# A perceiver block: the first key tile of a batch turned between two groups of key products, and copied ahead of the scaled probabilities

## The chip, the cores and the metric

The kernel runs on one core of a Trainium2 chip, as one program. The metric is the device time of a run in microseconds (us); lower is better. The kernel is written in five instruction streams, one for each engine (TensorE, VectorE, ScalarE, GpSimd, SyncE), which wait for one another by counting semaphores: `then_inc(s, 1)` counts up when an instruction is done, `wait_ge(s, n)` holds a stream, with all that is behind it, until the count is n.

## The reference

Three residual blocks over x (32 sequences of 32 rows, 512 wide): cross-attention to a context of 257 rows per sequence, a second attention-like block, and a mixture of 8 experts. The change touches the cross-attention alone:

```python
x = x + xattn(layernorm(x), ctx, mask, ...)
# in xattn: 8 heads of 64
q = (x @ Wq) ...; k, v = split(context @ Wkv)
q = per_head_ln(q, qn_w); k = per_head_ln(k, kn_w)
attn = softmax(where(mask, q @ k.T * SCALE, -inf))
out = (attn @ v) @ Wo
```

The kernel does not form v: it multiplies the probabilities with the context (the "context products") and applies the value weights afterwards. Products that need full precision are made from a high and a low part of each operand, three products in place of one (`split_products`).

## The kernel before

**Batches.** A batch b is one sequence, 32 in all, four to a tile of 128 rows; r is the batch's place in its tile (0 to 3). The 257 context rows of a sequence are two key tiles of 128 and a remainder of one row, which is done for all sequences at the start. The function `batch(tile, r, ...)` exists once in each engine's stream and is called 31 times with keys to make (`main`, b = 1 to 31; batch 0 is done in the opening), and once more for the last scores. The middle six tiles are a hardware loop. An iteration b does two things at once: it makes the normalised, transposed keys kT of batch b and the second half of the work of batch b-1 (scores, softmax, context products: `prev`). It also begins the key products of batch b+1 (`nxt`). The part of an iteration on each engine is fixed by the order in which it is written; nothing is planned at run time.

**TensorE in iteration b (L1758 on)**, in order:
1. scores of batch b-1 into pS (L1774, 16 small products), after the keys kT of batch b-1 are copied (kT0_set, kT1_set, k_rem);
2. key products of batch b, tile 1, into pK1 (`k_half`, L1632; 12 products of 512 columns);
3. in r=1 only, the output products of the tile before (`out_tile`, L1730);
4. nine of the twelve key products of batch b+1, tile 0, into pK0 (L1787);
5. four transposes of the scaled probabilities of batch b-1 into pP (L1802), after ScalarE's L841 (semaphore p_n);
6. the three products left of step 4 (L1805); in r=0 two transposes of the remainder's probabilities (L1810);
7. eight transposes of the normalised keys kn of batch b, four per tile, into pT0 and pT1 (L1818), after VectorE's k_norm of tile 1 (k_n); each four count k_t up by one;
8. 24 context products of batch b-1, twelve into pP and twelve into pV1 (L1834), after the low part of the probabilities pT (p_lo, VectorE L1254).

**ScalarE in iteration b (L820 on)**: high part of the context rows (L828); two exponentials (L834); square of the key products of tile 1 (`k_square`, L730); the two scaled probabilities (L841), after VectorE's p_scale; logarithm and exponential for the key norm of tile 1 (`k_root`, L734, L736); high part of the transposed probabilities pP into pT (L849); in r=0 a copy for the remainder (L852); `keys_copy` (L724 to L726), the copy of pT0 into the first half of kT, after the first count of k_t; high part of the context of b+2 (`ctx_high`, L722); square for b+1, tile 0; a copy of the first twelve context products into z (L871); `k_root` for b+1, tile 0; in r=0 four small copies (L878).

**VectorE in iteration b (L1217 on)**: mask (L1224, writes s_m) and maximum (L1227) of the scores; a transpose of blocks of context (L1106); p_den, p_inv, p_scale (L1235 to L1239), after the exponentials; p_rem (L1243); sum of squares and norm of key tile 1 (L1111, L1117); in r=1 a copy of the output products (L1214); low part of pT (L1254); the remainder's key column (L1261) and the copy of pT1 into the second half of kT (L1156), after k_t; sum and norm of tile 0 of b+1; a copy of the last twelve context products (L1270).

**GpSimd** makes low parts of context rows (L581) and of transposed context (L591), and copies queries (L587). **SyncE** issues the loads; neither has a wait on k_t in this loop (SyncE waits for its final count once, after the last batch).

Of the kernel before, what the change touches and what calls it, by code (L numbers as in the profile page):

```python
# [15 lines left out]
P = 128  # L16
# [21 lines left out]
def perceiver_block(nc, x, ctx, mask, xWq, xWkv, xWo, qn_w, kn_w, aWq, gq, bq, mq, vq, aWk, gk, bk, mk, vk,  # L38
# [6 lines left out]
    C = D // P  # L45
    BT = P // S
    MT = M // P
# [30 lines left out]
    with ExitStack() as es:  # L78
# [22 lines left out]
        ident = sb("ident", [P, P])  # L101
# [596 lines left out]
        def _(act):  # L698
# [29 lines left out]
            def k_square(b, t):  # L728
                act.wait_ge(k_mm, b * MT + t + 1)
                act.activation(sq[:, t], pKV[t][:, :], ACT.Square).then_inc(k_sq, 1)  # L730
# [89 lines left out]
            def batch(tile, r, main=True, prev=True, nxt=True, first=False, far=True):  # L820

                b = tile * BT + r
                u, pr = r % 2, (r - 1) % BT
                if main:
                    act.wait_ge(ctx_in[u], (tile * 2 + r // 2 + 1) * 16)
                    if not first:
                        act.wait_ge(pc_mm, (b - 1) * 2)
                    act.activation(ctxN[:, u, HI], ctx_raw[:, u], ACT.Copy).then_inc(cn_hi, 1)  # L828
                if prev:
                    act.wait_ge(sc_max, b)  # L830
                    if not first:
                        act.wait_ge(p_t, b - 1)
                    for g in range(G):
                        act.activation(prob[:, g, 0:M], s_m[:, g, 0:M], ACT.Exp, bias=neg_max[:, g:g + 1],  # L834
                                       accum_out=p_sum[:, g:g + 1]).then_inc(sc_exp, 1)
                if main:
                    k_square(b, 1)
                if prev:
                    act.wait_ge(sc_step, b * 3)
                    for g in range(G):  # L840
                        act.activation(prob[:, g, 0:MT * P], prob[:, g, 0:MT * P], ACT.Copy,  # L841
                                       scale=p_scale[:, g:g + 1]).then_inc(p_n, 1)
                if not main:
                    ln_root(TILES)
                if main:
                    k_root(b, 1)
                if prev:
                    act.wait_ge(p_t, b)
                    act.activation(pT[:, HI], pP[:, :, :], ACT.Copy).then_inc(p_hi, 1)  # L849
                    if r == 0:  # L850
                        act.wait_ge(p_rt, tile)
                        act.activation(pT_rem[0:3 * B, :], pV1[0:3 * B, 0:G * P], ACT.Copy).then_inc(p_rh, 1)  # L852
                if not main:
                    ln_root(TILES + 1)
                    out_high(4)
                    bn_root(0)
                if main:
                    keys_copy(b + 1)
                if far:
                    ctx_high(b + 2, u)  # L860
                if nxt:
                    k_square(b + 1, 0)
                if main and not nxt:
                    act.wait_ge(pc_mm, (b - 1) * 2 + 2)
                    out_high(2)

                if prev:
                    if r == 1 and not first:
                        act.wait_ge(o_mm, tile)
                    act.wait_ge(pc_mm, (b - 1) * 2 + 1)  # L870
                    act.activation(z[:, 2:4, :, pr, :], prob_ctx(1), ACT.Copy).then_inc(z1_set, 1)  # L871
                if nxt:
                    k_root(b + 1, 0)
                if prev:
                    if r == 0:
                        act.wait_ge(p_rh, tile)
                        for i in range(BT):
                            act.activation(rem_b[0:3 * B, :, i, :], pT_rem[0:3 * B, :].rearrange(  # L878
                                "p (h q) -> p h q", h=H), ACT.Copy, scale=sel[0:3 * B, bass.ds((tile - 1) * BT + i, 1)]).then_inc(p_rx, 1)
# [56 lines left out]
            for n in range(3 * TILES):  # L936
                w, t = divmod(n, TILES)
# [664 lines left out]
        def _(pe):  # L1602
# [140 lines left out]
            def z_product(n):  # L1743
# [11 lines left out]
                    pe.wait_ge(z_c, n - 2)  # L1755
                split_products(pe, pZ[n % 3][:, :], rows_of(xT, t), weight(w_a[:, w % 2]), C).then_inc(z_mm, 1)

            def batch(tile, r, main=True, prev=True, nxt=True, first=False):  # L1758


                b = tile * BT + r
                u, pr = r % 2, (r - 1) % BT
                if prev:
                    pe.wait_ge(kT0_set, b)
                    pe.wait_ge(kT1_set, b)
                    pe.wait_ge(k_rem, b)
                    pe.wait_ge(q_set, b)
                    if not first:
                        pe.wait_ge(sc_m, b - 1)
                    pe.nop(nofuse=True)  # L1770
                    for c in range(C):
                        for e in range(2):
                            half = slice(e * HD, (e + 1) * HD)
                            last = pe.matmul(pS[c * S:(c + 1) * S, e, 0:M], q_b[half, 1 - u, c, :],  # L1774
                                             kT[half, c, :], start=True, stop=True, tile_position=(e * HD, c * S))
                    last.then_inc(sc_mm, 1)
                if main:
                    pe.wait_ge(k_n, b * MT)
                    if first:
                        pe.wait_ge(q_n, TILES)  # L1780
                    k_half(b, 1, u)
                if r == 1 and not first:
                    out_tile(tile - 1)
                if nxt:
                    pe.wait_ge(k_n, b * MT + 1)
                    pe.wait_ge(ctx_lo, b + 2)
                    split_products(pe, pK0[:, :], ctx_rows(1 - u, 0), wk, C - 1, stop=False)  # L1787
                if main and not nxt:
                    pe.wait_ge(k_n, b * MT + 1)
                    project(0)  # L1790
                if not main:
                    project(1)
                    project(2)
                if prev:
                    pe.wait_ge(p_n, b * G)
                    if first:
                        pe.wait_ge(rem_act, 6)
                    else:
                        pe.wait_ge(z1_set, b - 1)
                    for t in range(MT):  # L1800
                        for g in range(G):
                            last = pe.transpose(pP[:, t, g * P:(g + 1) * P], prob[:, g, t * P:(t + 1) * P], ident[:, :])  # L1802
                    last.then_inc(p_t, 1)
                if nxt:
                    split_products(pe, pK0[:, :], ctx_rows(1 - u, 0), wk, C, start=False, first=C - 1).then_inc(k_mm, 1)  # L1805
                if prev and r == 0:
                    pe.wait_ge(p_rs, b)
                    pe.wait_ge(z0_set, b - 1)
                    for g in range(G):
                        last = pe.transpose(pV1[0:3 * B, g * P:(g + 1) * P], p_rem[:, g].rearrange("p k b -> p (k b)"), ident[:, :])  # L1810
                    last.then_inc(p_rt, 1)
                if not main:
                    project(3)
                if main:
                    pe.wait_ge(k_n, b * MT + 2)
                    for t in range(MT):
                        for c in range(C):
                            last = pe.transpose(pTT[t][:, c, :], kn[:, t, c * P:(c + 1) * P], ident[:, :])  # L1818
                        last.then_inc(k_t, 1)
                if prev:  # L1820
                    pe.wait_ge(cn_lo, b)
                    pe.wait_ge(p_lo, b)
                    for g in (1, 0):
                        for j in range(2):
                            c = 2 * g + j
                            o = pC[g][:, j * G * P:(j + 1) * G * P]
                            if (g, j) == (0, 0):
                                if not first:
                                    pe.wait_ge(z0_set, b - 1)
                                    if r == 0:  # L1830
                                        pe.wait_ge(p_rh, tile)
                                    if r == 1:
                                        pe.wait_ge(o_out, tile)
                            last = split_products(pe, o, lambda s, t: ctxN[:, 1 - u, s, t, c * P:(c + 1) * P],  # L1834
                                                  lambda s, t: pT[:, s, t, :], MT)
                        last.then_inc(pc_mm, 1)
# [228 lines left out]
```

## Time and profile before

| what | value |
|---|---|
| runs | 729.49 us median of 3 (724.91, 729.49, 729.84) |
| profiled execution | 726.1 us, span 724.0 us |
| TensorE products busy | 691.9 us (96%), 4651 |
| TensorE weight loads | 566.2 us (78%) |
| VectorE | 492.2 us (68%) |
| ScalarE | 443.3 us (61%) |
| GpSimd | 315.7 us (44%) |
| chain that ended last | TensorE 76%, VectorE 7%, DMA 5%, ScalarE 4% |

The span is what the trace covers; the execution's own time is 2.1 us longer. The batch loop lies between about 65 and 440 us of the span. TensorE's clock stands at nine tenths or more in 39 of the 40 slices of the span. In the trace a matmul has two records: a weight load (PEld) and the product (PE); products are pipelined, so three that follow one another take less than three times one.

### The profile page before, as it was taken

Reading aid. Unit: us, or ns where it says so; the run is one execution under the profiler, and the core shown is the slowest. Engines: PE = TensorE matmul, PEld = TensorE weight load, DVE = VectorE, ACT = ScalarE, POOL = GpSimd, SP = SyncE. Lnnn points to the kernel's source line nnn. Section 1 sums busy time; section 2 is a strip of 40 time slices with the busy share of each in tenths; the row PEclk is TensorE's granted clock in tenths of the full one; section 3 lists DMA queues with packets and bytes.
Section 4 is the critical chain, followed back from the end, with each engine's and each line's share of the span. In section 5 each row is a group of like instructions: output and inputs, shape, how many; then the busy total and the mean of one; then the engine's idle time right before and its main releaser. Section 6 shows DMA issues by size and latency. Waiting matters only on the chain.

```text
span 724.0 us, 14037 instructions
## 1 busy us (share of the span) xinstructions
PE 691.9 (96%) x4651; PEld 566.2 (78%) x4651; DVE 492.2 (68%) x869; ACT 443.3 (61%) x936; POOL 315.7 (44%) x243
## 2 busy tenths in 40 slices
PE   5888899999999999999999999999999989999996
PEld 4666778888888887888888878888788868888875
DVE  6766786766676767767667666877468766655573
ACT  4654676775776666856667655475564545565650
POOL 1473452544443434435353434744930024555534
PEclk9999999999999999999999999999999989999999
DMA  9963535352533443434524306630126367666549
GB/s 259 206 121 99 157 74 147 73 146 72 145 109 108 104 114 94 123 91 127 141 77 116 104 1 188 212 130 8 59 65 226 115 206 209 111 116 107 104 72 345
DMA packets 95063, 91.98 MB, mean 127 GB/s; under 512 B 11440, under 2 KB 68784, under 8 KB 95024
## 3 DMA queue, kind: packets, MB, share of 16 engines
q1 hardware_dynamic: 89728, 79.14, 39.6%
q0 software_dynamic: 4720, 11.27, 8.5%
q10 hardware_dynamic: 576, 1.05, 0.4%
q8 instruction: 23, 0.38, 0.2%
q14 instruction: 16, 0.13, 0.1%
HBM read 71.52 MB, written 19.92 MB: 126 GB/s over the span
## 4 chain that ended last, share of the span: by engine, by line
PE 76%; DVE 7%; DMA 5%; SPq 4%; ACT 4%; issue 2%; POOL 2%; DVEq 0%; ACTq 0%; POOLq 0%
PE pK L33 40%; PE pV L33 10%; PE pP L33 8%; PE pV L1730 5%; PE pT L1818 4%; PE pP L1802 2%; PE pS L1774 2%; DMA mask_f<-in_mask_BxSxS_bk_dram 2%; DMA fin<-total 1%; PE pT L1963 1%; SPq L409 1%; DMA big<-x_rows,idx_x 1%; SPq L421 1%; DVE ctxR L1106 1%; POOL mask_f L577 1%
## 5 line engine op out<-in xcount | busy, mean ns | idle before, releaser
L33 PE MATMUL pK<-parts 128*128 128x512 f32 x744 | 188.5, 400 | 1.9 <-DVE kn L1117 1.0
L33 PEld LDWEIGHTS pK<-parts 128*128 128x128 f32 x744 | 134.4, 188 | 41.2 <-issue 13.6
L591 POOL TENSOR_TENSOR parts<-ctxR,parts 128x1024 fp32r<-128x1024 f32 x32 | 77.0, 2407 | 186.6 <-ACT parts L722 186.6
L581 POOL TENSOR_TENSOR parts<-big,parts 128x1024 fp32r<-128x1024 f32 x32 | 77.9, 2434 | 29.0 <-ACT parts L828 28.9
L1117 DVE TENSOR_TENSOR kn<-pK,head_rs 128x512 f32<-128x512 f32 x62 | 42.9, 692 | 40.5 <-ACT head_rs L736 40.5
L33 PE MATMUL pK<-w,lhs 128*128 x276 | 69.1, 399 | 0.5 <-DVE lhs L1539 0.2
L1111 DVE TENSOR_REDUCE head_ss<-sq 128x8 f32<-128x512 f32 x62 | 42.5, 685 | 28.7 <-ACT sq L730 28.7
L33 PEld LDWEIGHTS pK<-w,lhs 128*128 128x128 f32 x276 | 50.3, 188 | 11.4 <-issue 1.8
L834 ACT ACTIVATE prob<-s_m,neg_max 128x257 f32<-128x257 f32 x64 | 32.2, 506 | 38.1 <-DVE neg_max L1227 38.1
L33 PE MATMUL pP<-pT,parts 128*128 128x256 f32 x384 | 52.7, 286 | 0.0
L1555 DVE TENSOR_TENSOR w_p<-big,w_p 128x1024 fp32r<-128x1024 f32 x22 | 27.0, 1226 | 37.8 <-ACT w_p L1031 37.8
L33 PE MATMUL pV<-pT,parts 128*128 128x256 f32 x384 | 50.1, 279 | 0.0
L677 POOL DMA_INDIRECT total<-big,idx x20 | 31.7, 1586 | 40.9 <-ACT big L1045 40.9
L33 PEld LDWEIGHTS pP<-pT,parts 128*128 128x128 f32 x384 | 47.2, 188 | 1.8 <-issue 0.2
L33 PEld LDWEIGHTS pV<-pT,parts 128*128 128x128 f32 x384 | 47.3, 188 | 0.0
L33 PE MATMUL pK<-w_p,parts 128*128 128x512 f32 x156 | 41.0, 414 | 2.1 <-DVE w_p L1126 1.9
L33 PE MATMUL pK<-w_a,xT_hi 128*128 128x512 f32 x128 | 40.2, 395 | 0.0
L841 ACT ACTIVATE prob<-prob,p_scale 128x256 f32<-128x256 f32 x64 | 29.1, 502 | 15.8 <-DVE p_scale L1239 13.1
L849 ACT ACTIVATE pT<-pP 128x512 fp32r<-128x512 f32 x32 | 19.1, 598 | 32.0 <-PE pP L1802 32.0
L671 POOL DMA_INDIRECT big<-x_rows,idx_x x23 | 26.7, 1162 | 25.0 <-DVE idx_x L1511 10.6
L33 PEld LDWEIGHTS pK<-w_p,parts 128*128 128x128 f32 x156 | 30.0, 197 | 9.5 <-DVE w_p L1126 2.3
L1254 DVE TENSOR_TENSOR pT<-pP,pT 128x512 fp32r<-128x512 f32 x32 | 22.1, 692 | 22.3 <-ACT pT L849 20.5
(331 smaller groups left out, 1521.6 us busy)
## 6 DMA issues: line engine op xcount, KB each, us to landing
big<-in_ctx_dram SPq DMA_DIRECT2D x32, 512.0 KB, 4.7
big<-in_ctx_dram SPq DMA_DIRECT2D x120, 128.0 KB, 2.7
total<-zero SPq DMA_DIRECT2D x32, 256.0 KB, 4.8
w_raw<-in_L_ffn_w_dram SPq DMA_DIRECT2D x16, 512.0 KB, 7.0
big<-in_L_ffn_w_dram SPq DMA_DIRECT2D x8, 512.0 KB, 5.7
fin<-total SPq DMA_DIRECT2D x8, 512.0 KB, 7.7
total<-big SPq DMA_DIRECT2D x8, 256.0 KB, 2.8
x_rows<-big SPq DMA_DIRECT2D x8, 256.0 KB, 2.0
```

The lines of the kernel that those rows point to most:

```text
L33: last = pe.matmul(out, lhs(a, c), rhs(b, c), start=start and c == first and n == 0, stop=stop and c == chunks - 1 and n == 2)
L581: nc.gpsimd.tensor_tensor(ctxN[:, u, LO], ctx_raw[:, u], ctxN[:, u, HI].bitcast(F32), ALU.subtract).then_inc(cn_lo, 1)
L591: nc.gpsimd.tensor_tensor(ctxT[:, u, LO], ctxR[u][:, :, :], ctxT[:, u, HI].bitcast(F32), ALU.subtract).then_inc(ctx_lo, 1)
L671: nc.gpsimd.indirect_dma_start(xg[:, j % 2, :], None, x_rows[:, :], bass.IndirectOffsetOnAxis(idx_x[:, j:j + 1], 0), bounds_check=T - 1).t ...
L677: nc.gpsimd.indirect_dma_start(total[:, :], bass.IndirectOffsetOnAxis(idx[:, j:j + 1], 0), y_sb[:, j % 2, :], None, bounds_check=5 * T - 1 ...
L834: act.activation(prob[:, g, 0:M], s_m[:, g, 0:M], ACT.Exp, bias=neg_max[:, g:g + 1], accum_out=p_sum[:, g:g + 1]).then_inc(sc_exp, 1)
L841: act.activation(prob[:, g, 0:MT * P], prob[:, g, 0:MT * P], ACT.Copy, scale=p_scale[:, g:g + 1]).then_inc(p_n, 1)
L1111: nc.vector.tensor_reduce(head_ss[:, t], heads(sq[:, t]), AX.X, ALU.add).then_inc(k_ss, 1)
L1117: tt(heads(kn[:, t]), heads(pKV[t][:, :]), per_head(head_rs[:, t]), ALU.mult).then_inc(k_n, 1)
L1555: tt(w2_buf(j)[:, LO], w2_all[:, bass.ds(e, 1)].rearrange("p e c n -> p (e c) n"), w2_buf(j)[:, HI].bitcast(F32), ALU.subtract).then_inc(w ...
L1730: last = pe.matmul(o, weights, rows[:, e * C + c].rearrange("p b q -> p (b q)"), start=k == 0, stop=k == C, tile_position=(0, e * HD))
L1818: last = pe.transpose(pTT[t][:, c, :], kn[:, t, c * P:(c + 1) * P], ident[:, :])
```

## The change

In TensorE's stream the eight transposes of step 7 are split. A new function `keys_turn(t)` makes the four of key tile t and counts k_t up. `keys_turn(0)` now stands right behind step 2, ahead of the output products and of the nine key products, with a wait for the norm of tile 0 alone; `keys_turn(1)` stays at step 7, behind the wait for tile 1. In ScalarE's stream the copy of pT0 (`keys_copy`) moves up, from behind L849 (and L852) to between the square of tile 1 and the two scaled probabilities. Nothing else moves, and the number of instructions on each engine, leaving waits aside, is the same.

```diff
--- before.py
+++ after.py
@@ -835,6 +835,8 @@
                                        accum_out=p_sum[:, g:g + 1]).then_inc(sc_exp, 1)
                 if main:
                     k_square(b, 1)
+                if main:
+                    keys_copy(b + 1)
                 if prev:
                     act.wait_ge(sc_step, b * 3)
                     for g in range(G):
@@ -854,8 +856,6 @@
                     ln_root(TILES + 1)
                     out_high(4)
                     bn_root(0)
-                if main:
-                    keys_copy(b + 1)
                 if far:
                     ctx_high(b + 2, u)
                 if nxt:
@@ -1755,6 +1755,11 @@
                     pe.wait_ge(z_c, n - 2)
                 split_products(pe, pZ[n % 3][:, :], rows_of(xT, t), weight(w_a[:, w % 2]), C).then_inc(z_mm, 1)
 
+            def keys_turn(t):
+                for c in range(C):
+                    last = pe.transpose(pTT[t][:, c, :], kn[:, t, c * P:(c + 1) * P], ident[:, :])
+                last.then_inc(k_t, 1)
+
             def batch(tile, r, main=True, prev=True, nxt=True, first=False):
 
 
@@ -1779,6 +1784,9 @@
                     if first:
                         pe.wait_ge(q_n, TILES)
                     k_half(b, 1, u)
+                if main:
+                    pe.wait_ge(k_n, b * MT + 1)
+                    keys_turn(0)
                 if r == 1 and not first:
                     out_tile(tile - 1)
                 if nxt:
@@ -1813,10 +1821,7 @@
                     project(3)
                 if main:
                     pe.wait_ge(k_n, b * MT + 2)
-                    for t in range(MT):
-                        for c in range(C):
-                            last = pe.transpose(pTT[t][:, c, :], kn[:, t, c * P:(c + 1) * P], ident[:, :])
-                        last.then_inc(k_t, 1)
+                    keys_turn(1)
                 if prev:
                     pe.wait_ge(cn_lo, b)
                     pe.wait_ge(p_lo, b)
```

## Rows read from the trace of the kernel before

**Rows 1.** Busy time by stretch, scores to scores: r=1, r=2, r=3, r=0 (us, count, clock, DMA).

```profile
303.90:319.24 15.34, 15.34 (x157) 13.10 (x157) 9.57 (x16) 9.49 (x22) 5.21 (x4) 1.00 0.33 87
319.24:329.85 10.61, 10.61 (x78) 8.68 (x77) 7.94 (x15) 7.56 (x17) 4.95 (x4) 1.00 0.47 121
329.85:340.58 10.73, 10.73 (x77) 8.66 (x77) 7.94 (x15) 7.67 (x18) 5.06 (x4) 1.00 0.42 122
340.58:351.37 10.79, 10.79 (x80) 8.92 (x79) 7.95 (x15) 8.04 (x19) 5.06 (x4) 1.00 0.45 122
```

**Rows 2.** The list of waits, TensorE: total us, times, longest.

```profile
PE pP L1802 <- ACT prob L841: 4.8, 5, 1.7
...
PEld pP L1802 <- ACT prob L841: 12.7, 23, 2.2
...
PEld pT L1818 <- DVE kn L1117: 5.9, 17, 0.6
```

**Rows 3.** Order of time, r=1: start, us, engine, line, what, idle before.

```profile
311.97 2.34 PE L33 MATMUL pK<-parts 128*128 128x512 f32 x9
...
314.14 0.60 PE L1802 MATMUL pP<-ident,prob 128*128 128x128 f32 x4
...
314.50 0.94 PE L33 MATMUL pK<-parts 128*128 128x512 f32 x3
314.78 0.60 ACT L849 ACTIVATE pT<-pP 128x512 fp32r<-128x512 f32 x1 [3.71 <-PE pP L1802]
...
315.27 1.04 PE L1818 MATMUL pT<-ident,kn 128*128 128x128 f32 x8
315.41 0.69 DVE L1254 TENSOR_TENSOR pT<-pP,pT 128x512 fp32r<-128x512 f32 x1 [2.50 <-ACT pT L849]
...
316.25 1.65 PE L33 MATMUL pP<-pT,parts 128*128 128x256 f32 x12
```

**Rows 4.** The same view, r=3.

```profile
329.44 0.30 ACT L734 ACTIVATE head_log<-head_ss,bias 128x8 f32<-128x8 f32 x1 [0.27 <-DVE head_ss L1111]
...
329.85 0.67 PE L1774 MATMUL pS<-kT,q_b 64*32 64x257 f32 x16
...
330.44 5.05 PE L33 MATMUL pK<-parts 128*128 128x512 f32 x21
...
331.15 2.42 POOL L581 TENSOR_TENSOR parts<-big,parts 128x1024 fp32r<-128x1024 f32 x1 [0.23 <-ACT parts L828]
331.31 0.68 DVE L1224 SCALAR_TENSOR_TENSOR s_m<-mask_f,pS 128x514 f32<-128x514 f32 x1
...
333.75 0.58 ACT L730 ACTIVATE sq<-pK 128x512 f32<-128x512 f32 x1
333.88 0.16 DVE L1235 SCALAR_TENSOR_TENSOR p_den<-neg_max,p_sum 128x2 f32<-128x2 f32 x1
...
334.47 0.91 ACT L841 ACTIVATE prob<-prob,p_scale 128x256 f32<-128x256 f32 x2
...
335.43 0.66 PE L1802 MATMUL pP<-ident,prob 128*128 128x128 f32 x4
...
336.12 0.60 ACT L849 ACTIVATE pT<-pP 128x512 fp32r<-128x512 f32 x1 [0.20 <-PE pP L1802]
...
336.75 0.69 DVE L1254 TENSOR_TENSOR pT<-pP,pT 128x512 fp32r<-128x512 f32 x1
...
337.40 0.60 ACT L726 ACTIVATE kT<-pT 128x512 f32<-128x512 f32 x1 [0.68 <-PE pT L1818]
...
337.59 1.65 PE L33 MATMUL pP<-pT,parts 128*128 128x256 f32 x12
```

**Rows 5.** The same view, transposes of the probabilities in r=2 and r=0.

```profile
324.73 0.62 PE L1802 MATMUL pP<-ident,prob 128*128 128x128 f32 x4
...
346.18 0.66 PE L1802 MATMUL pP<-ident,prob 128*128 128x128 f32 x4
```

**Rows 6.** The same view, p_den of the second batch.

```profile
83.04 1.54 DVE L1235 SCALAR_TENSOR_TENSOR p_den<-neg_max,p_sum 128x2 f32<-128x2 f32 x1
```

## The prediction

> **What bounds the kernel now.** I read four views in this order: the list of waits, the busy time by stretch, the order of time in one batch of each kind, and two batches near the start. I call a batch by r, its place in its tile of four, and by b from 1 to 31; S is the start of its scores, P that of the transposes of its probabilities (L1802), C that of its context products.
>
> The stretches between the scores of four neighbouring batches last 15.34, 10.61, 10.73 and 10.79 us, with TensorE busy in all of it at the full granted clock, 1.00, the 2.4 GHz level [rows 1]. The batch r=1 is the long one, since the output products stand in it. So TensorE's queue sets the pace: a step off it pays only if it takes a wait out of it, and a step put into it costs.
>
> The waits that the change could remove are small. TensorE's products stood still before L1802 for 4.8 us in only 5 batches; its weight loads 12.7 us in 23, mostly while earlier products still ran, and 5.9 us before the key transposes [rows 2]. In r=3 the products begin at 330.44 and take 5.05; a last one that began 0.39 (the length of one) before their end would let the transposes begin 0.22 later, as in r=1 (311.97 + 2.34 - 0.39 = 313.92, transposes at 314.14). That is 335.32; they began at 335.43. So 0.11 us of real wait, though the loads show 0.36 there [rows 3, 4].
>
> The second thing to see is a race at the end of each batch. After P the probabilities go through ScalarE's copy (L849) and VectorE's low part (L1254), and only then may the context products begin. Meanwhile TensorE does three key products and all eight key transposes. In r=1: P 314.14, low part ready at 316.10 (315.41 + 0.69), context products 316.25 [rows 3]. In r=3: P 335.43, ready 337.44, products 337.59 [rows 4]. The eight transposes end just when the low part is ready: they are the cover of this chain.
>
> **The change, part by part.**
>
> *Four transposes go in front, between two groups of key products.* The kernel has the same insertion already: four transposes between nine and three products. Products cost (5.05 - 2.34) / 12 = 0.226 each, so twelve in one piece take 2.34 + 3 x 0.226 = 3.02; with the four between them they last from 311.97 to 314.50 + 0.94 = 315.44, 3.47 [rows 3, 4]. Insertion: **0.45 us**. Lower bound 0.36, start to start of the four (314.50 - 314.14); upper 0.55, if the restart is counted in full (314.50 against 311.97 + 9 x 0.22). I take 0.45, it counts both ends. Their input, the normalised tile 0, is made at the end of the batch before, and the target is free once the scores have begun: no wait is expected there. Behind them are queued, in r=1, the output products, in all batches the next tile's products, then P.
>
> The trace shows four such transposes 0.36 apart in all, about 0.09 each, plus a restart. The Trainium skill (TensorE: Matmul & The Clock Gate, Back-to-back issue gap) gives about 81 ns for a 128-column product in a stream of loads and products. By that the insertion would be estimated at 0.32 instead of 0.45; it is a rival below.
>
> *The four behind the probabilities go.* The old tail from P to C is 2.11 us in r=1 (316.25 - 314.14) [rows 3]. Eight transposes there take 316.25 - 315.27 = 0.98; four less save some 0.44, so TensorE would be ready at P + 1.67. But the low part is ready at P + 1.96 (r=1) or P + 2.01 (r=3), and the products start 0.06 to 0.10 later. I take P + 2.07. From C to the next S are 340.58 - 337.59 = 2.99, so P to S becomes 5.06. Now it is 319.24 - 314.14 = 5.10 (r=1), 329.85 - 324.73 = 5.12 (r=2), 340.58 - 335.43 = 5.15 (r=3), 351.37 - 346.18 = 5.19 (r=0) [rows 1, 3, 4, 5]. The removal gives back 0.04, 0.06, 0.09 and 0.13 only: the rest turns into a wait of the context products for pT, some 0.3 to 0.4 us in every batch.
>
> *ScalarE's copy of 0.60 us goes ahead of the scaled probabilities.* It used to wait 0.68 for TensorE and then run [rows 4]. Ahead of L841 there is a gap that hides part of it: the square starts at 333.75, L841 at 334.47, 0.72 later, of which the square itself fills some 0.57. With the copy between them L841 comes about 1.17 after the square: +0.45. Queued behind it on ScalarE are L841, the root for key tile 1 and L849; TensorE waits for L841 and then L849. Against that, with the copy gone from its old place, the next square and sum come earlier. The logarithm at 329.44 no longer waits 0.27 for the sum, and VectorE, which works through the key norm and a copy before the mask step at 331.31 (scores over at 329.85 + 0.67 = 330.52), starts that up to 0.30 earlier [rows 4]. Net on ScalarE +0.15: L841 ends at S + 5.53 + 0.15 = S + 5.68 (334.47 + 0.91 - 329.85 = 5.53). TensorE gets to P at S + 0.59 + 5.05 + 0.45 - 0.17 = S + 5.92. So TensorE decides by 0.15 to 0.2, and the copy is free; without the earlier start ScalarE would give P at S + 6.03, nearly the same. No DMA and no queue of SP or POOL is moved; POOL's low part of ctx only comes about 1 us earlier.
>
> *Sum.* P moves by +0.45 (r=1), +0.43 (r=2: 319.24 + 5.92 = 325.16 against 324.73), +0.34 (r=3: 335.77 against 335.43), +0.32 (r=0: 346.50 against 346.18) [rows 3 to 5]. Less what is given back: +0.41, +0.37, +0.25, +0.19. The 23 regular batches b = 5 to 27 hold six each of the first three and five of the last: 6 x 1.03 + 5 x 0.19 = 7.1. The eight at the ends: b=28 0.2, b=29 0.4, b=31 (no wait at P) 0.45. In b=2, 3, 30 VectorE's p_scale is late anyway (b=2: L1235 lasts 1.54 [rows 6]) and both the copy and the transposes fit into the wait: -0.05 each. In b=1 and 4 TensorE waits for L841, which comes later: 0.3 each. Together 1.5. Total **+8.6 us**.
>
> The profiled execution took 726.1 (span 724.0), so it becomes 734.7. The runs shown have the median 729.49, between 724.91 and 729.84, so the execution lies 3.4 below the median; from the middle of the runs, some 728, I come to **737 us**. Bounds: insertion 0.36 gives about +6, insertion 0.55 with no earlier start on the softmax side about +13.
>
> **Rivals.**
>
> 1. *The split costs less than its row, or the tail gives back more.* If the four cost 0.32, every P that TensorE sets moves 0.13 less, 28 x 0.13 = 3.6: +5, 733. If the low part did not hold the context products, the tail would return 0.44 per batch against 0.45 spent: +0.3, 728. For it: the work is only moved. Against it: P to ready is 1.96 and 2.01 in two kinds of batch, all of it made of instructions that the change does not touch. These two together: 0.37, both inside 1%.
>
> 2. *Faster.* The place is P: if keys ready early took away the waits before L1802 and the transposes cost nothing in the shadow of weight loads. The price at most: 4.8 us of product waits and about 0.3 per regular batch of small waits at P and at the keys, 23 x 0.3 = 7: 726.1 - 12 = 714; half of it is likelier, 720. It decides where L841 ends later than S + 5.92 now; it ends at S + 5.53. Hence 0.06. The scores' side can't be advanced much either: POOL's L581 runs until 331.15 + 2.42 = 333.57, and in b=2 a tiny VectorE step stretched to 1.54 beside it [rows 4, 6]. The Trainium skill (SBUF — State Buffer, SBUF: two separate sides) says that VectorE and GpSimd lock a shared port and the loser blocks; the trace agrees with those 1.54 us.
>
> 3. *Slower still.* ScalarE's copy catches the transposes late (they end at about S + 3.44 + 0.66 = S + 4.1, the square at 333.75 + 0.58 - 0.30, S + 4.2) or p_den, now some 0.3 earlier, lands behind POOL. Each adds 0.2 to 0.3 on L841 in the 17 batches r=2, 3, 0: +4 to +5 more, 742. Chance 0.12.
>
> The forecast itself: 0.45.
>
> **How the numbers follow.** A measurement of this kernel tells about 1%, 7.3 us, from no change. The forecast of +8.6 lies just beyond; some of its own spread falls within: 0.45 gives 0.38 slower and 0.07 same. Rival 1 gives 0.32 same and 0.05 slower, rival 3 0.12 slower, rival 2 0.06, of which 0.05 faster. Slower 0.55, same 0.40, faster 0.05. The range reaches from rival 1's lower end, 728.5, to rival 3's, 742.
>
> **What the changed profile would show.** Scores to scores near 15.75, 10.98, 10.98 and 10.98 us. Four key transposes about S + 3.4, the products after them 0.45 later. L726 on ScalarE right behind the square, without idle time. L841 near S + 4.8. L849 and L1254 as far behind P as now. Context products with a new wait for pT (L1254) of 0.3 to 0.4, which is the step that makes the loss; if that wait is missing and C follows P by 1.7, I am wrong and nothing changes. If nine products follow the first twelve with less than 0.36 between, the insertion was overpriced. If P waits for L841 by more than 0.2, rival 3 holds.

## The result, and the profile after

The changed kernel is slower, by about 1%. Its runs have the median 734.31 us against 728.79 of the runs beside them, ratio 1.0087 with a 95% interval of 1.0054 to 1.012 (the ratios in this text are not quotients of medians; that of these two is 1.0076). Two later rounds of it gave 1.0109 (1.0081 to 1.0138) and 1.0105 (1.0085 to 1.0125). The forecast was 737, with 728.5 to 742. The profiled execution has a span of 732.7 us against 724.0, +8.7, where the sum said +8.6.

First the busy time by stretch of the changed kernel, from scores to scores, r=1, 2, 3, 0; the columns are those of [rows 1].

```profile
309.06:324.74 15.68, 15.32 (x157) 13.07 (x157) 9.41 (x17) 8.98 (x21) 5.68 (x5) 1.00 0.31 84
324.74:335.79 11.05, 10.68 (x77) 8.78 (x76) 7.86 (x16) 7.41 (x17) 5.08 (x3) 1.00 0.45 118
335.79:346.85 11.06, 10.69 (x78) 8.78 (x77) 7.75 (x16) 7.46 (x17) 5.09 (x3) 1.00 0.43 119
346.85:357.80 10.95, 10.80 (x79) 8.89 (x79) 7.76 (x16) 8.06 (x19) 4.46 (x2) 1.00 0.45 119
```

Each batch is longer than in [rows 1], and TensorE is no longer busy in all of it: 0.36 or 0.37 us are missing in r=1, 2 and 3, and 0.15 in r=0. The clock is the same. The list of waits of the changed kernel (total us, times, longest) names the missing piece; L1810 is now what L1802 was, L843 what L841 was.

```profile
PE pP L33 <- DVE pT L1254: 9.4, 25, 1.0
...
PE pP L1810 <- ACT prob L843: 1.9, 2, 1.5
```

The list of the kernel before has no line like the first. The wait is 0.32 to 0.37 us in 23 batches of r=1, 2 and 3. In r=0 no such wait shows but for 0.15 us in batch 4: there two transposes of the remainder's probabilities stand in the tail as well. Before the probabilities TensorE waits less, 1.9 us in place of the 4.8 of [rows 2]. Next the order of time in r=1, which answers to [rows 3].

```profile
317.57 2.34 PE L33 MATMUL pK<-parts 128*128 128x512 f32 x9
...
319.74 0.60 PE L1810 MATMUL pP<-ident,prob 128*128 128x128 f32 x4
...
320.10 0.95 PE L33 MATMUL pK<-parts 128*128 128x512 f32 x3
320.38 0.60 ACT L851 ACTIVATE pT<-pP 128x512 fp32r<-128x512 f32 x1 [4.55 <-PE pP L1810]
...
320.89 0.60 PE L1760 MATMUL pT<-ident,kn 128*128 128x128 f32 x4
321.01 0.69 DVE L1254 TENSOR_TENSOR pT<-pP,pT 128x512 fp32r<-128x512 f32 x1 [2.50 <-ACT pT L851]
...
321.85 1.60 PE L33 MATMUL pP<-pT,parts 128*128 128x256 f32 x12 [0.36 <-DVE pT L1254]
```

The chain P, L851, L1254, context products has kept its length: 321.85 - 319.74 = 2.11, as in [rows 3]. Four transposes fewer stand in it, and the products wait for the low part instead. The last view of this kernel is r=2; it answers to [rows 4] and [rows 5].

```profile
324.74 0.66 PE L1779 MATMUL pS<-kT,q_b 64*32 64x257 f32 x16
...
325.33 3.02 PE L33 MATMUL pK<-parts 128*128 128x512 f32 x12
...
325.90 0.68 DVE L1224 SCALAR_TENSOR_TENSOR s_m<-mask_f,pS 128x514 f32<-128x514 f32 x1
...
328.19 0.60 PE L1760 MATMUL pT<-ident,kn 128*128 128x128 f32 x4
...
328.39 0.60 ACT L730 ACTIVATE sq<-pK 128x512 f32<-128x512 f32 x1
...
328.54 2.31 PE L33 MATMUL pK<-parts 128*128 128x512 f32 x9
...
328.88 0.59 ACT L726 ACTIVATE kT<-pT 128x512 f32<-128x512 f32 x1
...
329.36 0.91 ACT L843 ACTIVATE prob<-prob,p_scale 128x256 f32<-128x256 f32 x2
...
330.70 0.60 PE L1810 MATMUL pP<-ident,prob 128*128 128x128 f32 x4
...
332.80 1.65 PE L33 MATMUL pP<-pT,parts 128*128 128x256 f32 x12 [0.37 <-DVE pT L1254]
```

The 21 key products with the four transposes in them last from 325.33 to 328.54 + 2.31 = 330.85, 5.52 us against 5.05: the insertion costs 0.47. P is at S + 5.96, set by TensorE (L843 ends at 330.27, with no wait shown at P). P to context products is 2.10.

To compare kernels I also use the length of the loop in their profiles, from the scores of batch 1 to those of batch 32: 371.5 us before, 379.0 after, +7.5. The other 1.2 us of the +8.7 lie outside it: the first scores come 0.9 later (66.31 against 65.38), and what follows the loop takes 0.3 more. The loop is steadier than the whole run, for a reason given at the end.

### The profile page after: what moved, and what is told of

The parts are those of the page before. It is cut to its first block, busy times and chain, and to the rows that moved or that the text cites. A ratio compares the mean times of both kernels' runs of the same rounds, so it can differ in the third digit from the quotient of the medians.

```text
span 732.7 us, 14037 instructions
## 1 busy us (share of the span) xinstructions
PE 694.1 (95%) x4651; PEld 568.7 (78%) x4651; DVE 484.7 (66%) x869; ACT 437.3 (60%) x936; POOL 315.9 (43%) x243
## 3 DMA queue, kind: packets, MB, share of 16 engines
q10 hardware_dynamic: 576, 1.05, 0.4%
## 4 chain that ended last, share of the span: by engine, by line
PE 75%; DVE 6%; ACT 4%; SPq 4%; DMA 4%; POOL 4%; issue 2%; DVEq 0%; ACTq 0%; POOLq 0%
PE pK L33 38%; PE pV L33 11%; PE pP L33 9%; PE pV L1730 4%; DVE pT L1254 3%; ACT pT L851 3%; PE pS L1779 2%; PE pP L1810 2%; PE pT L1760 2%; DMA mask_f<-in_mask_BxSxS_bk_dram 2%; PE pT L1968 1%; SPq L409 1%; DMA big<-x_rows,idx_x 1%; SPq L421 1%; POOL mask_f L577 1%
## 5 line engine op out<-in xcount | busy, mean ns | idle before, releaser
L33 PE MATMUL pK<-parts 128*128 128x512 f32 x744 | 195.0, 404 | 0.9 <-POOL parts L591 0.9
L33 PEld LDWEIGHTS pK<-parts 128*128 128x128 f32 x744 | 132.7, 188 | 38.8 <-DVE kn L1117 7.9
L581 POOL TENSOR_TENSOR parts<-big,parts 128x1024 fp32r<-128x1024 f32 x32 | 77.8, 2431 | 52.3 <-ACT parts L828 52.3
L851 ACT ACTIVATE pT<-pP 128x512 fp32r<-128x512 f32 x32 | 19.2, 599 | 47.0 <-PE pP L1810 47.0
L1254 DVE TENSOR_TENSOR pT<-pP,pT 128x512 fp32r<-128x512 f32 x32 | 22.1, 692 | 31.4 <-ACT pT L851 31.4
L1760 PE MATMUL pT<-ident,kn 128*128 128x128 f32 x248 | 37.3, 273 | 1.0 <-DVE kn L1117 1.0
L730 ACT ACTIVATE sq<-pK 128x512 f32<-128x512 f32 x62 | 36.7, 591 | 1.5 <-PE pK L33 0.2
```

The costliest lines, as they stand in the source:

```text
L33: last = pe.matmul(out, lhs(a, c), rhs(b, c), start=start and c == first and n == 0, stop=stop and c == chunks - 1 and n == 2)
L581: nc.gpsimd.tensor_tensor(ctxN[:, u, LO], ctx_raw[:, u], ctxN[:, u, HI].bitcast(F32), ALU.subtract).then_inc(cn_lo, 1)
L1254: tt(pT[:, LO], pP[:, :, :], pT[:, HI].bitcast(F32), ALU.subtract).then_inc(p_lo, 1)
```

## Experiments

| kernel | ratio to before | 95% interval | loop, us |
|---|---|---|---|
| the change | 1.0087, 1.0109, 1.0105 | see above | 379.0, 379.0, 379.4 |
| split on TensorE only | 1.0139, 1.0099 | 1.0116 to 1.0162, 1.0066 to 1.0131 | 379.5, 379.0 |
| copy twice | 1.0044 | 1.0025 to 1.0063 | 374.7 |
| cover back | 1.0129 | 1.0100 to 1.0159 | 379.4 |
| change, high part first | 0.9989 | 0.9969 to 1.0008 | 368.9 |
| before, high part first | 1.0019 | 1.0006 to 1.0032 | 372.4 |
| one piece | 1.0085 | 1.0058 to 1.0112 | 376.4 |
| mixed, high part first | 0.9947 | 0.9928 to 0.9966 | 367.4 |
| the same, copy late | 0.9948 | 0.9921 to 0.9974 | 367.7 |

The runs below were made in three rounds on three chips, each with runs of the kernel before beside them (medians 726.54, 725.95 and 727.27 us), and each ratio goes by those of its own round.

My theory: the four transposes in front cost TensorE their full time, and the four taken away at the tail give nothing back, because the chain that makes pT sets the start of the context products. The main rival: ScalarE's copy, which now delays the scaled probabilities.

**Split on TensorE only.** TensorE's stream as in the change; ScalarE, against the changed kernel:

```diff
                 if main:
                     k_square(b, 1)
-                if main:
-                    keys_copy(b + 1)
...
+                if main:
+                    keys_copy(b + 1)
                 if far:
                     ctx_high(b + 2, u)
```

> Only TensorE's half of the change: the four transposes of key tile 0 go between the key products, ScalarE's copy stays behind the high part of the probabilities. My theory (TensorE sets P, the four in front cost 0.45 us, the four taken from the tail give back almost nothing because the context products then wait for pT): the same loss as the full change, P at S + 5.9, context products at P + 2.1, +7 to +9 us on the kernel before, ratio 1.008 to 1.012. Rival (the copy ahead of the scaled probabilities makes the loss): back to the kernel before, ratio 1.000.

The loop takes as long as with the whole change. Its list of waits has the same new line:

```profile
PE pP L33 <- DVE pT L1254: 9.4, 25, 1.0
...
PE pP L1681 <- DMA wv<-in_L_xattn_Wkv_dram: 8.5, 1, 8.5
```

But the ratio was 1.0139, above what I had expected. The second line is from the opening: 8.5 us for the weights wv, where the changed kernel's profile shows 0.7. So the kernel ran once more.

> The split-only kernel once more, beside the changed kernel's next run and on the same chip, since its first time (ratio 1.014) lay 3 us above what its loop says (379.5 us from the scores of batch 1 to those of batch 32, against 379.0 in the changed kernel). Expected from the loop: ratio 1.009 to 1.012, the same as the changed kernel. Rival (ScalarE's early copy is worth 3 us outside the places I have looked at): again 1.013 or more, and at least 0.3% above the changed kernel.

Now it has 1.0099, and the changed kernel beside it, run with this expectation, 1.0105:

> The changed kernel as the partner of the run above: ratio 1.009 to 1.011.

The whole loss is in TensorE's half of the change, and the rival falls. That the opening raised the first ratio is likely but not shown: the one profile is of the slowest of its six runs (745.05 us, their median is 737.92).

The same profile shows what the early copy does to ScalarE. Order of time, r=2:

```profile
332.84 0.66 PE L1779 MATMUL pS<-kT,q_b 64*32 64x257 f32 x16
...
334.00 0.68 DVE L1224 SCALAR_TENSOR_TENSOR s_m<-mask_f,pS 128x514 f32<-128x514 f32 x1
...
337.16 0.91 ACT L841 ACTIVATE prob<-prob,p_scale 128x256 f32<-128x256 f32 x2
...
338.80 0.60 PE L1810 MATMUL pP<-ident,prob 128*128 128x128 f32 x4
```

The scaled probabilities are over at S + 5.23 here and at S + 5.53 with the early copy (329.36 + 0.91 - 324.74), yet P is at S + 5.96 in both. So the copy does delay them, by 0.30 in r=2 and by 0.42 in r=3, and TensorE is later still.

**Copy twice.** The kernel before, and on ScalarE ahead of the scaled probabilities:

```diff
                 if main:
                     k_square(b, 1)
+                if main and prev:
+                    act.activation(kT[:, :, 0:P], pTT[0][:, :, :], ACT.Copy)
```

> TensorE's order of the kernel before; ScalarE copies the last keys a second time, 0.60 us, between the square and the scaled probabilities (the copy in the old place stays; the second writes what already stands there). It prices the copy where no transposes stand in front of it. My theory: L841 comes 0.45 later, hidden in r=1 and in the early batches that wait for p_scale, on the path in 17 regular batches and some three at the ends: +8 to +9 us, ratio 1.011 to 1.012; then the copy is free in the changed kernel only because the transposes delay TensorE by as much. Rival (ScalarE has room there): +0 to +2 us, ratio under 1.003.

Less than half of what I expected: ratio 1.0044 against 1.011 to 1.012, loop +3.2. Order of time, r=3:

```profile
332.45 0.67 PE L1776 MATMUL pS<-kT,q_b 64*32 64x257 f32 x16
...
336.34 0.58 ACT L730 ACTIVATE sq<-pK 128x512 f32<-128x512 f32 x1
...
336.82 0.58 ACT L839 ACTIVATE kT<-pT 128x512 f32<-128x512 f32 x1
...
337.30 0.90 ACT L843 ACTIVATE prob<-prob,p_scale 128x256 f32<-128x256 f32 x2
...
338.25 0.66 PE L1804 MATMUL pP<-ident,prob 128*128 128x128 f32 x4 [0.15 <-ACT prob L843]
```

The copy shows a length of 0.58 but costs ScalarE 0.48 from start to start, and so does the square before it. The scaled probabilities come 0.96 after the square, where they came 0.72 after it in [rows 4]: +0.24, not +0.45. In the changed kernel the same distance is 329.36 - 328.39 = 0.97. P is at S + 5.80 here, +0.22 on [rows 4]. The copy has a price, but it is smaller than that of the transposes, and in the changed kernel TensorE's later P hides it.

**Cover back.** The changed kernel, and key tile 0 turned a second time at the tail:

```diff
                     pe.wait_ge(k_n, b * MT + 2)
+                    for c in range(C):
+                        pe.transpose(pTT[0][:, c, :], kn[:, 0, c * P:(c + 1) * P], ident[:, :])
                     keys_turn(1)
```

> The changed kernel with four more transposes: key tile 0 is also turned again in its old place behind the probabilities, so the tail has its eight transposes as before, and TensorE does 124 transposes more than either kernel. My theory (behind the probabilities four transposes stand in the shadow of the chain pP, L849 and L851, L1254): no loss against the changed kernel in r=1, 2, 3 (0.0 to 0.05 each), 0.2 in r=0, so +1 to +3 us on the changed kernel, ratio to the kernel before 1.010 to 1.013, and no wait of the context products for L1254. Rival (every group costs its own time wherever it stands): 31 x 0.44, +14 us more, ratio 1.028.

Order of time, r=3:

```profile
343.91 0.60 PE L1810 MATMUL pP<-ident,prob 128*128 128x128 f32 x4
...
345.05 0.60 PE L1825 MATMUL pT<-ident,kn 128*128 128x128 f32 x4
345.17 0.69 DVE L1254 TENSOR_TENSOR pT<-pP,pT 128x512 fp32r<-128x512 f32 x1 [0.57 <-ACT pT L851]
345.49 0.60 PE L1760 MATMUL pT<-ident,kn 128*128 128x128 f32 x4
346.01 1.65 PE L33 MATMUL pP<-pT,parts 128*128 128x256 f32 x12
```

P to context products is 2.10 with eight transposes and no wait, as it was 2.10 with four and a wait. 124 transposes more lengthen the loop by 0.4 us at most; the changed kernel's own three loops differ by as much. This is the plainest proof of the cover: the four at the tail were free, so taking them away could not pay. The ratio, 1.0129, is some 1.5 us over the loop's account (+7.9 us); the interval reaches down to 1.0100.

**High part first.** The changed kernel; in r=1, 2, 3 the context products begin with the four that need only pT's high part, into the bank (pV1) that VectorE does not read for the low part:

```diff
                     pe.wait_ge(cn_lo, b)
+                    if ahead:                       # main and r != 0
+                        ...
+                        pe.wait_ge(p_hi, b)
+                        context(0, 0, high, True, False)
                     pe.wait_ge(p_lo, b)
```

> The changed kernel, but in r=1, 2, 3 the context products begin with the four that need only the high part of pT (they wait for ScalarE's copy, not for VectorE's low part) and into the bank that does not hold the transposed probabilities. It takes the new wait away. My theory: context products at P + 1.7 in place of P + 2.1, -0.35 to -0.43 us in 24 batches, -8 to -10 us on the changed kernel, ratio to the kernel before 0.997 to 1.001. Rival (the loss is the insertion's alone and the wait only took the place of idle time that would come anyway): it stays within 2 us of the changed kernel, ratio 1.006 to 1.009.

Order of time, r=3:

```profile
338.73 0.60 PE L1810 MATMUL pP<-ident,prob 128*128 128x128 f32 x4
...
339.86 0.60 PE L1760 MATMUL pT<-ident,kn 128*128 128x128 f32 x4
340.00 0.69 DVE L1254 TENSOR_TENSOR pT<-pP,pT 128x512 fp32r<-128x512 f32 x1 [0.30 <-ACT pT L851]
340.22 0.72 PE L1832 MATMUL pV<-pT,parts 128*128 128x256 f32 x4
...
340.77 1.65 PE L1832 MATMUL pP<-pT,parts 128*128 128x256 f32 x12
```

The context products begin 1.49 after P, while the low part is still being made, and the other twenty begin when it is done (340.00 + 0.69 = 340.69, products at 340.77). So TensorE is free 0.6 us before it may start in the changed kernel, and fills that time with four products. The loop is 10.1 us shorter than the changed kernel's, r=1 by 0.43 us each time and r=2 and 3 by some 0.5. The loss is gone with the wait, and the insertion is still in. Whether the products had waited for the low part itself or for the bank from which VectorE makes it is not separated: both come free with L1254. The control says whether that order is better in itself:

> The kernel before with the context products of r=1, 2, 3 begun by the four that need only the high part. The control for the run that took the new wait away. My theory: in the kernel before, eight transposes already cover the chain of pT, no wait is there to be taken: P to context products stays 2.1, loop within 2 us of before, ratio 0.997 to 1.001. Rival (that order of the context products is faster in itself): as much as in the changed kernel, -10 us, ratio 0.986.

It is not. On the kernel before it lengthens the loop by 1.0 us, and the ratio, 1.0019, lies just above the expected range. Order of time there, r=3:

```profile
336.09 0.66 PE L1802 MATMUL pP<-ident,prob 128*128 128x128 f32 x4
...
337.36 1.09 PE L1818 MATMUL pT<-ident,kn 128*128 128x128 f32 x8
...
338.21 0.72 PE L1827 MATMUL pV<-pT,parts 128*128 128x256 f32 x4
```

P to context products is 2.12 in r=3 and r=2, the eight transposes fill it. In r=1 it falls from 2.11 to 1.92, and that batch is 0.17 shorter (15.17 against 15.34): there the low part held the products back a little even before. In r=2 the batch is 0.2 longer, and P comes at S + 5.70 in place of S + 5.49; why, I have not traced. So the same edit gives -10.1 behind four transposes and +1.0 behind eight: its gain is that of the uncovered chain.

Beside these ran the changed kernel:

> The changed kernel itself, beside the others on one chip. From its loop (scores of batch 1 to scores of batch 32 take 7.5 us longer than before): ratio 1.009 to 1.011. It also gives the spread that the opening brings in (the wait of TensorE for the weights wv was 0.7 to 8.5 us in the profiles so far). Rival to my reading of the split-only kernel's 1.014: if the changed kernel stays at 1.009 or below here, ScalarE's early copy does help by some 3 us.

It met the loop's account, and the early copy is not worth 3 us.

**One piece.** The kernel before with the twelve key products together ahead of P, all transposes behind one another, and the high part first:

```diff
-                    split_products(pe, pK0[:, :], ctx_rows(1 - u, 0), wk, C - 1, stop=False)
+                    split_products(pe, pK0[:, :], ctx_rows(1 - u, 0), wk, C).then_inc(k_mm, 1)
```

> The kernel before with all twelve key products of the next tile in one piece ahead of P, all transposes behind one another (four of the probabilities, eight of the keys), and the context products begun by the high part. If TensorE's own work is the floor, P comes 0.68 later (S + 6.15) and the context products 1.34 to 1.5 after it: r=1 15.2, r=2 and 3 10.5 to 10.6, r=0 10.75, loop 3 us shorter than before, ratio 0.995 to 0.998. Rival (the three products between the transposes are needed as cover too): the eight transposes end before the high part or the norm of tile 1 is there, 0.2 to 0.4 more per batch, ratio 1.004 to 1.012.

The rival came. The three products between the transposes are cover too. List of waits, and order of time in r=3:

```profile
PE pT L1816 <- DVE kn L1117: 5.3, 17, 0.5
```

```profile
339.67 0.60 PE L1802 MATMUL pP<-ident,prob 128*128 128x128 f32 x4
...
340.50 1.09 PE L1816 MATMUL pT<-ident,kn 128*128 128x128 f32 x8 [0.23 <-DVE kn L1117]
...
341.35 0.71 PE L1825 MATMUL pV<-pT,parts 128*128 128x256 f32 x4
```

P is where I put it (S + 6.17), but the transposes now wait 0.23 for the norm of tile 1, and the context products begin 1.68 after P. The dearest batch is r=0, which cannot begin by the high part: 11.17 us against 10.79, with a wait of 0.23 to 0.26 for L1254. The r=1 batch, where that norm is early, still took 15.49 and not 15.2. Order of time there:

```profile
318.21 0.60 PE L1802 MATMUL pP<-ident,prob 128*128 128x128 f32 x4
...
319.47 0.69 DVE L1254 TENSOR_TENSOR pT<-pP,pT 128x512 fp32r<-128x512 f32 x1 [3.17 <-ACT pT L849]
319.58 0.70 PE L1825 MATMUL pV<-pT,parts 128*128 128x256 f32 x4
...
320.22 1.68 PE L1825 MATMUL pP<-pT,parts 128*128 128x256 f32 x12
```

The first four products begin 1.37 after P, as I expected. The others follow 0.64 later and not 0.55 as in the changed kernel with the high part first, just behind the low part (319.47 + 0.69 = 320.16). That is 0.09 of the miss; the rest of it is open.

**Mixed.** The changed kernel with the high part first, and r=0 in the order of before on both engines:

```diff
-                if main:
+                if main and r:
                     keys_copy(b + 1)
...
-                if main:
+                if main and r:
                     pe.wait_ge(k_n, b * MT + 1)
                     keys_turn(0)
...
+                    if not r:
+                        keys_turn(0)
                     keys_turn(1)
```

> The changed kernel with the high part first, and r=0 left in the order of the kernel before on TensorE and ScalarE, since r=0 (where the context products can't begin by the high part) took 11.0 to 11.1 in the run before against 10.79. Expected: r=0 10.79, r=1 15.25, r=2 and 3 10.55, loop 371.5 - 4.5 = 367, 1.8 less than with the change in all r: ratio 0.994 to 0.998, the best so far. If r=0 stays at 11.0, its loss comes from something else than the order of the turns.

This one beats both kernels, by half a per cent: 722.35 us against 725.95, ratio 0.9947 with an interval that ends at 0.9966. Its batches r=1, 2, 3, 0 take about 15.26, 10.55, 10.53 and 10.84 us. The last run puts the copy back behind L849 in every r:

> The best kernel so far (split turns in r=1, 2, 3, high part first) with ScalarE's copy in its old place in every r. With the wait for pT gone, TensorE alone should set the pace, and the place of the copy should not matter: P at S + 5.95, loop 367 to 369 us (367.4 with the early copy), ratio 0.994 to 0.998. Rival (the early copy is what keeps L841 and L849 in time): P later than S + 6.05 in r=2 or 3 or a wait before the context products, loop over 370.

The place of the copy makes no difference: 0.9948, and P stays at S + 5.95 to 6.00 in r=2 and 3.

## Why the prediction was right

The forecast named the sign, the place and, in the loop, nearly the size (+8.6 us forecast, +7.5 measured). By its steps:

| step | forecast | measured |
|---|---|---|
| insertion of four transposes | 0.45 | 0.47 (5.52 against 5.05) |
| P after S in r=2, 3 | 5.92, by TensorE | 5.96, by TensorE |
| L841 over after S in r=2, 3 | 5.68 | 5.53 |
| P to context products | 2.07 | 2.11, 2.10 |
| new wait for L1254 | 0.3 to 0.4, in every batch | 0.36, 0.37 in r=1, 2, 3; none in r=0 |
| copy on ScalarE | L841 +0.45 after the square | +0.25 (0.97 against 0.72) |
| r=1, 2, 3, 0 | 15.75, 10.98, 10.98, 10.98 | 15.68, 11.05, 11.06, 10.95 |
| 23 regular batches | +7.1 | +7.7 (281.7 against 274.1) |
| eight batches at the ends | +1.5 | -0.2 |

**The insertion** was priced by the kernel's own row of the same pattern, and that held. From the first transpose to the next product it is 0.35 of the 0.47 (328.54 - 328.19). By the figure of the Trainium skill (TensorE: Matmul & The Clock Gate, Back-to-back issue gap), about 81 ns for each product of 128 columns in a stream, the estimate was 0.32 in all; that is near the 0.35 and too low for the 0.47, and the measurement decides.

**The tail** was the step that made the sign. Rival 1, which let the tail give 0.44 back, fails on the wait in the list and on the two runs that add to the cover or take the need for it away. The forecast put TensorE's readiness with four transposes at P + 1.67. The regular batches of the changed kernel with the high part first show 1.48 to 1.54. The 0.98 that the forecast read for eight transposes in r=1 held some hidden wait for the low part: with the high part first they take 0.79 (315.83 to 316.62 in the control). It changed nothing in the sum, because the low part is later than either.

**The copy** was mis-sized: I added up durations where ScalarE starts the next copy before the last has ended. The earlier start of the mask step that was to make up for a part of it did come, at S + 1.16 in r=2 (325.90 - 324.74) where it was S + 1.32, and at S + 1.05 in r=3 where it was S + 1.46, but not for the reason given: with the copy left in its old place it starts at the same S + 1.16 (334.00 - 332.84) and, in r=3, S + 1.04. So it comes from TensorE's half of the change. Neither changed the sum, since TensorE set P with room to spare, but the first made the expectation of the copy-twice run wrong by more than a factor of two and rival 3 likelier than it was. Rival 2 (faster) had no place: P never waited by much.

**The ends** were mis-sized as well. Batches 2, 4 and 30 became shorter (11.81 to 11.00, 11.79 to 11.56, 11.39 to 11.06), where I had given back 0.05 in two and taken 0.3 in one. In batch 2, p_den lasts 0.68 in place of the 1.54 of [rows 6]: GpSimd's L581 starts at 82.04, 1.76 after the scores at 80.28, and not 2.93 after them (82.14 against 79.21), so that it is over sooner; in both traces p_den ends 0.02 after it. I give the cause for this batch alone. The regular batches were 0.6 dearer than forecast in all (r=2 and 3 more, r=1 less, since its tail gave back 0.10 and not 0.04).

**The total** is right to 0.1 us by luck. The sum is one of the loop, and there it was +7.5 against 8.6; 1.2 us from outside the loop filled the gap. The 737 is 3 us too high: it adds a distance between the profiled execution and the median which the changed kernel does not have (734.83 and 734.31). The prediction also took 1%, 7.3 us, as what a measurement can tell. Between medians the first round has 5.5 us, under that line, the later ones 8.3 and 7.2; all three intervals lie above 1.000. Two small slips of its text: rival 1's lower end is 728 in one place and 728.5 in the other, and the 0.36 us of the loads at P in r=3 is in the trace but not in the rows that it names.

## What to carry to other kernels

Before work is moved off an engine that is always busy, look at what chain of other engines runs beside it where it stands: if the two end together, the work is cover, and moving it turns it into a wait while its price is paid again in the new place. A cheap test is to put the work back as idle duplicates and see that nothing gets slower. Where a chain is to lose its cover, first start its consumer with the operands that are ready early; here that edit is worth 10 us behind four transposes and costs 1 us behind eight.

## What the runs showed of the hardware

On ScalarE a square and a copy of 128 x 512 out of PSUM show durations of 0.58 us each, but the copy starts 0.48 after the square and the next instruction 0.48 after the copy (336.34, 336.82, 337.30).

The opening moves the whole run by several microseconds. TensorE's wait for wv was 0.7 to 8.5 us in the profiles of these kernels, and the first scores stood between 65.4 and 74.1 us. In the first split-only profile the mean granted clock fell in the opening (columns as in [rows 1]; the clock is the third number from the end):

```profile
25.00:30.00 5.00, 4.47 (x26) 3.52 (x24) 3.07 (x8) 3.27 (x8) 2.65 (x4) 1.00 1.12 308
30.00:35.00 5.00, 0.00 (x0) 0.00 (x0) 4.13 (x8) 3.13 (x8) 2.81 (x4) 0.83 1.31 80
35.00:40.00 5.00, 2.05 (x3) 1.02 (x4) 0.69 (x1) 0.10 (x1) 1.41 (x2) 0.50 0.69 74
```

The 0.50 is the 1.2 GHz level. TensorE had stood still before it, in the 8.5 us wait that ends at 37.95. The loop takes 379.5 us in this profile and 379.0 in the second. The length of the loop, which does not contain the opening, agreed within 0.5 us between profiles of the same kernel, for the two kernels that have more than one.
